# A new order of work in a fused attention and expert kernel: the next rows' transposes in two visits around the last up block, and the sixth expert product behind the query product

## The chip, the cores and the metric

The kernel runs on one core of a Trainium2 chip. The metric is the device time of one execution in microseconds (us). Runs of the kernel before gave 1293.66, 1293.72 and 1294.25 us, median 1293.72 us. Engine names are those of the profile: PE (matmul), PEld (its weight load), DVE (vector), ACT (scalar), POOL (GpSimd), SP (queues of the DMAs).

## The reference

For each of 32 batch rows ("turns" below) of 256 tokens by 256 features and 77 context tokens:

```
latents = layernorm(x); ctx = masked context
q = LN(latents) @ W_q;  k, v = [LN(ctx), LN(latents)] @ W_kv      # 333 keys, 4 heads of 64
x1 = x + softmax(rms(q) rms(k)^T / 8) v @ W_out + b_out
h  = layernorm(x1)
cw = router(h)                        # sigmoid, best of 2 groups, 2 of 8 experts
out = x1 + shared(h) + sum_e cw[e] * relu(h @ up[e])^2 @ down[e]  # all 8 experts are computed
```

All of it is in float32. The kernel splits each operand of a large product into a high and a low part (`_hi`, `_lo`) and adds three products: hi*hi, hi*lo, lo*hi.

## The kernel before

Five engines each run a program of their own, written out by hand, and meet only in semaphores. A turn `step(b, ...)` holds the attention of row b, the router and experts of row b-1 (`ffn(...)`, `high`, `add`, `routing`, `low`) and the layer norm and projections of row b+1 (the lines under `if following`). No scheduler moves anything: an engine does what its `step` lists, in that order, and stops at a `wait_ge` until it is met. 31 turns have experts, 30 of those also prepare a next row. After the last turn a drain computes the experts of the last row alone.

What the names stand for on PE: `transpose_k`, `sum_q_squares` open the turn; `up(p)` (p = 0 to 5) computes two hidden blocks into bank p % 2 of `up_ps`; `shared` and `down(e)` are the products back to 256 features in `down_ps`; `score_pair`, `transpose_probs(u)`, `probs_times_v` are the attention; `transpose_ln(b + 1)` turns the normalized next rows `x_hat`, `c_hat` into `up_ps` (feature half ft = 0 in bank 0, ft = 1 in bank 1); `spread_inverse` transposes the softmax's inverse sums; `project_kv`, `project_out`, `project_q` are the projections and `transpose_x2` opens the second layer norm's output to the experts.

The chain of an `up` block runs over four engines: ACT reads the bank (`relu_sb`, line 657) and squares it (`relu2`, 662), DVE rounds it to `hid_hi` (981, `high(p)`), POOL subtracts (`hid_lo`, 1176, `low(p)`), then PE may use it in `down`. `down(e)` for e = 2, 3 needs `high(3)` and `low(3)`. Its result is added up by DVE (`add(e)`, 996), and `down(e)` waits until `add(e - 2)` has freed the bank.

The chain of the next rows: DVE takes the statistics (`layer_norm1`, 740 to 758), POOL the inverse root (`rstd_first`, 1133, which stands behind `low(3)` on POOL), DVE writes `x_hat`, `c_hat` (`normalize1`, 765, 767), PE transposes them (275, 276), ACT applies gain and bias (`ln_full`, 576), DVE and POOL split (775, 1144), and `project_kv` starts.

At the turn's end DVE computes `x1` from the output projection (872), its statistics, the key norms (795, 800), `x2_hat` (891), the normalized keys `k_rms` (810), which `transpose_k` of the next turn waits for, and `x2_lo` (898), which `up(0)` waits for.

## Time and profile before

| | before |
|---|---|
| median of three runs | 1293.72 us |
| the profiled execution's own time | 1296.0 us |
| its span, first to last instruction | 1294.1 us |
| PE busy | 1218.2 us (94% of the span) |
| DVE busy | 1048.6 us (81%) |
| ACT busy | 752.5 us (58%) |
| POOL busy | 539.6 us (42%) |
| mean granted clock of PE | 0.989 |
| one turn in the middle (start of `transpose_k` to the next) | 38.96 us |

The span is what the sums of this document are made against; the profiled execution took 1.9 us more than its span. Busy time of PE is modelled from pipelined matmuls, so a PE that shows 94% is not idle for the other 6% alone. The granted clock of PE was nine tenths or more in every slice of the page but the second (7) and the last (8), so it tells no stretch of the middle apart. The turns repeat each other to a few hundredths of a microsecond. One turn, 645.34 to 684.30 us, stands for all in what follows.

### The profile page before, as it was taken

The numbers are of one execution on the slowest core, as the hardware profiler recorded it, in microseconds if no ns is written. First come the engines' busy times: TensorE is split into PE (matmuls) and PEld (weight loads), VectorE is DVE, ScalarE is ACT, GpSimd is POOL, SyncE is SP. The second block draws the span as 40 slices with busy tenths as digits, with TensorE's granted clock in tenths as the row PEclk, the third lists the DMA queues.
The fourth block names the chain that finished last, engine by engine and source line by source line (L and its number), as shares of the span: only waits on it lengthen the run. The fifth ranks groups of instructions, "written<-read, shape, count | busy, mean of one in ns | idle before, by whom it ended". The sixth has DMA issues, their size and how long they took to land.

```text
span 1294.1 us, 29594 instructions
## 1 busy us (share of the span) xinstructions
PE 1218.2 (94%) x10176; PEld 1105.8 (85%) x10176; DVE 1048.6 (81%) x3561; ACT 752.5 (58%) x1733; POOL 539.6 (42%) x477
## 2 busy tenths in 40 slices
PE   3799999999999999999999999999999999999987
PEld 2589888889888888888888888888888888988876
DVE  3778888888888888888888888888888888888875
ACT  3566556666555666556656556656556566555652
POOL 3244454344344344444344444344444344344332
PEclk9799999999999999999999999999999999999998
DMA  4000000000000000000000000000000000000000
GB/s 145 12 12 21 20 20 10 12 21 20 21 20 16 5 21 20 20 20 20 2 21 20 20 20 20 2 21 20 20 20 20 2 21 21 20 20 20 2 9 17
DMA packets 28227, 25.84 MB, mean 20 GB/s; under 512 B 6640, under 2 KB 27536, under 8 KB 28080
## 3 DMA queue, kind: packets, MB, share of 16 engines
q1 hardware_dynamic: 27744, 23.83, 5.8%
q8 instruction: 82, 1.34, 0.4%
q0 software_dynamic: 336, 0.14, 0.2%
q14 instruction: 65, 0.53, 0.1%
HBM read 15.57 MB, written 8.39 MB: 19 GB/s over the span
## 4 chain that ended last, share of the span: by engine, by line
PE 60%; DVE 18%; issue 14%; ACT 7%; POOL 1%; DMA 1%; DVEq 0%; POOLq 0%; ACTq 0%
PE up_ps L261 8%; PE up_ps L263 7%; PE attn_ps L370 7%; PE up_ps L262 7%; PE attn_ps L356 4%; PE attn_ps L261 4%; PE down_ps L261 4%; DVE masked L830 4%; PE attn_ps L262 3%; PE attn_ps L263 3%; ACT relu L662 3%; PE down_ps L262 3%; PE down_ps L263 3%; ACT relu_sb L657 3%; DVE acc L996 2%
## 5 line engine op out<-in xcount | busy, mean ns | idle before, releaser
L1176 POOL TENSOR_TENSOR hid_lo<-relu,hid_hi 128x512 fp32r<-128x512 f32 x192 | 247.3, 1288 | 417.1 <-DVE hid_hi L981 417.1
L261 PE MATMUL down_ps<-down_hi,hid_hi 128*128 128x256 f32 x768 | 236.1, 307 | 5.1 <-issue 3.0
L996 DVE SCALAR_TENSOR_TENSOR acc<-down_ps,route_w,acc 128x256 f32<-128x256 f32 x512 | 221.6, 475 | 13.9 <-PE down_ps L263 13.5
L261 PE MATMUL up_ps<-x_hi,up_hi 128*128 128x256 f32 x768 | 227.7, 296 | 3.4 <-issue 0.4
L262 PE MATMUL down_ps<-down_lo,hid_hi 128*128 128x256 f32 x768 | 216.3, 282 | 0.0
L263 PE MATMUL down_ps<-down_hi,hid_lo 128*128 128x256 f32 x768 | 216.1, 281 | 0.0
L262 PE MATMUL up_ps<-x_lo,up_hi 128*128 128x256 f32 x768 | 216.1, 281 | 0.0
L263 PE MATMUL up_ps<-x_hi,up_lo 128*128 128x256 f32 x768 | 215.7, 281 | 0.0
L617 ACT ACTIVATE probs<-masked,neg_max,q_scale 128x333 f32<-128x333 f32 x256 | 168.3, 658 | 73.7 <-DVE neg_max L837 73.7
L657 ACT ACTIVATE relu_sb<-up_ps 128x512 f32<-128x512 f32 x192 | 114.6, 597 | 105.8 <-PE up_ps L263 99.2
L981 DVE CAST hid_hi<-relu 128x512 fp32r<-128x512 f32 x192 | 124.6, 649 | 56.6 <-ACT relu L662 56.4
L261 PEld LDWEIGHTS down_ps<-down_hi,hid_hi 128*128 128x128 f32 x768 | 145.7, 190 | 19.5 <-issue 17.6
L261 PEld LDWEIGHTS up_ps<-x_hi,up_hi 128*128 128x128 f32 x768 | 146.4, 191 | 18.1 <-issue 13.2
L262 PEld LDWEIGHTS down_ps<-down_lo,hid_hi 128*128 128x128 f32 x768 | 145.9, 190 | 1.2
L262 PEld LDWEIGHTS up_ps<-x_lo,up_hi 128*128 128x128 f32 x768 | 146.0, 190 | 0.0
L263 PEld LDWEIGHTS up_ps<-x_hi,up_lo 128*128 128x128 f32 x768 | 145.8, 190 | 0.0
L263 PEld LDWEIGHTS down_ps<-down_hi,hid_lo 128*128 128x128 f32 x768 | 145.4, 189 | 0.0
L624 ACT ACTIVATE up_stage<-attn_ps 111x384 f32<-111x384 f32 x256 | 117.8, 490 | 43.6 <-PE attn_ps L356 43.5
L1133 POOL TENSOR_TENSOR rstd<-var,minus_half 128x2 f32<-128x2 f32 (+1 forms) x64 | 51.4, 803 | 204.2 <-DVE var L884 191.7
L662 ACT ACTIVATE relu<-relu_sb 128x512 f32<-128x512 f32 x192 | 121.3, 632 | 6.1
L356 PE MATMUL attn_ps<-ident,probs 128*111 128x128 f32 x768 | 117.1, 283 | 7.9 <-DVE row_max L830 7.9
L830 DVE CUSTOM_DVE_ANT_0 masked<-attn_ps,mask_row 128x333 f32<-128x333 f32 x256 | 118.1, 498 | 0.3 <-issue 0.3
(147 smaller groups left out, 2821.5 us busy)
## 6 DMA issues: line engine op xcount, KB each, us to landing
x_in<-in_x SPq DMA_DIRECT2D x32, 256.0 KB, 2.8
out<-acc SPq DMA_DIRECT2D x32, 256.0 KB, 2.1
c_in<-in_ctx SPq DMA_DIRECT2D x32, 77.0 KB
up_stage<-in_up_t SPq DMA_DIRECT2D x1, 1536.0 KB, 12.9
down_stage<-in_down_t SPq DMA_DIRECT2D x1, 1536.0 KB, 15.3
mask_in<-in_mask SPq DMA_DIRECT2D x32, 9.6 KB, 2.6
w_stage<-in_w_kv SPq DMA_DIRECT2D x1, 512.0 KB, 5.8
w_stage<-in_w_q SPq DMA_DIRECT2D x1, 256.0 KB, 5.0
```

The lines of the kernel that those rows point to most:

```text
L261: nc.tensor.matmul(out_ap, s_hi, m_hi, start=first, stop=False)
L262: nc.tensor.matmul(out_ap, s_hi, m_lo, start=False, stop=False)
L263: return nc.tensor.matmul(out_ap, s_lo, m_hi, start=False, stop=last)
L356: last = nc.tensor.transpose(attn_ps[0:KC, u % PT_RING, c * P:(c + 1) * P], probs[:, u, c * KC:(c + 1) * KC], ident[:])
L617: nc.scalar.activation(probs[:, u, :], masked[:, u, :], ACT.Exp, bias=neg_max[:, u:u + 1], scale=q_scale[:, u:u + 1], accum_out=row_sum[:, ...
L624: nc.scalar.activation(probs_t[:, u % PT_SB, :], attn_ps[0:KC, u % PT_RING, 0:CH * P], ACT.Copy).then_inc(pt_done, 1)
L657: nc.scalar.activation(relu_sb[:, p % 2, :], up_ps[:, p % 2, :], ACT.Relu).then_inc(relu_done, 1)
L662: nc.scalar.activation(relu2[:, p % 2, :], relu_sb[:, p % 2, :], ACT.Square).then_inc(relu2_done, 1)
L830: nc.vector.tensor_tensor_reduce(masked[:, u, :], attn_ps[:, u % SCORE_RING, 0:KEYS], mask_row[:], 1.0, -MASKED, ALU.add, ALU.max, row_max ...
L981: nc.vector.tensor_copy(hid_hi[:, p % HID_RING, :], relu2[:, p % 2, :]).then_inc(hid_hi_done, 1)
L996: nc.vector.scalar_tensor_tensor(acc[:, t, :], down_ps[:, (e + 1) % 2, t * D:(t + 1) * D], route_w[:, t, e:e + 1], acc[:, t, :], ALU.mult, ...
L1176: nc.gpsimd.tensor_tensor(hid_lo[:, p % HID_RING, :], relu2[:, p % 2, :], hid_hi[:, p % HID_RING, :], ALU.subtract).then_inc(hid_lo_done, 1)
```

## The change

Nothing is computed differently but two things are cut finer: the output projection of token half t now goes to bank t of `up_ps`, signals each half, and DVE adds the residual in two halves (`residual_half`); and `transpose_ln` and `ln_full` take one feature half at a visit. Everything else is order. On PE: the router ahead of `up(1)`; score pairs 0 and 1 together and 2 and 3 together; `up(2)`, `up(3)` adjacent; probability transposes 0, 1, 2 together, 4, 5, 6 together; `down(1)` ahead of `probs_times_v`; the next rows' first half transposed ahead of `up(5)`, the second half behind `down(3)`; two of three `project_kv` ahead of `project_out`; `down(5)` behind `project_q`, which now waits for the first residual half. ACT, DVE and POOL follow with orders of their own.

```diff
-            def transpose_ln(b, experts):
+            def transpose_ln(b, ft, experts):
+                if ft == 0:
+                    pe.wait_ge(x_hat_done, b + 1)
...
             def project_q(b):
-
+                if not (isinstance(b, int) and b == 0):
+                    pe.wait_ge(x1_done, (b - 1) * T + 1)
...
-                    last = split_product(up_ps[:, 1, t * D:(t + 1) * D], (at_hi[:, k, cols], at_lo[:, k, cols]),
+                    last = split_product(up_ps[:, t, 0:D], (at_hi[:, k, cols], at_lo[:, k, cols]),
...
-                if t == T - 1:
-                    last.then_inc(out_ps, 1)
+                last.then_inc(out_ps, 1)
...
                 ffn("up", 0)
-                ffn("up", 1)
                 if experts:
                     router(f)
+                ffn("up", 1)
                 score_pair(b, 0, experts)
+                score_pair(b, 1, experts)
                 ffn("up", 2)
-                score_pair(b, 1, experts)
                 ffn("up", 3)
                 score_pair(b, 2, experts)
+                score_pair(b, 3, experts)
                 ffn("shared", 0)
                 ffn("shared", 1)
-                score_pair(b, 3, experts)
                 transpose_probs(b, 0)
                 transpose_probs(b, 1)
+                transpose_probs(b, 2)
                 ffn("down", 0)
-                transpose_probs(b, 2)
                 transpose_probs(b, 3)
                 ffn("up", 4)
+                ffn("down", 1)
                 probs_times_v(b, 0)
                 probs_times_v(b, 1)
-                ffn("down", 1)
                 transpose_probs(b, 4)
                 transpose_probs(b, 5)
+                transpose_probs(b, 6)
                 ffn("down", 2)
+                if following:
+                    transpose_ln(b + 1, 0, experts)
                 ffn("up", 5)
-                transpose_probs(b, 6)
                 ffn("down", 3)
                 if following:
-                    transpose_ln(b + 1, experts)
+                    transpose_ln(b + 1, 1, experts)
...
                 if following:
                     project_kv(b + 1, 1)
-                ffn("down", 5)
+                    project_kv(b + 1, 2)
                 project_out(b, 0, following)
                 project_out(b, 1, following)
                 if following:
-                    project_kv(b + 1, 2)
                     project_kv(b + 1, 0)
                     project_q(b + 1)
+                ffn("down", 5)
                 ffn("down", 6)
...
+            def residual_half(b, t):
+                if t == 0:
+                    dve.wait_ge(x_res_done, b + 1)
+                dve.wait_ge(out_ps, b * T + t + 1)
+                nc.vector.tensor_tensor(x1[:, t, :], up_ps[:, t, 0:D], x_res[:, t, :], ALU.add).then_inc(x1_done, 1)
+                dve.wait_ge(x1_done, b * T + t + 1)
+                nc.vector.bn_stats(stats2[:, t, :], x1[:, t, :]).then_inc(ln2_step, 1)
...
                 high(0)
-                high(1)
                 routing(0)
...
                 mask_scores(b, 0, first)
                 mask_scores(b, 1, first)
-                routing(1, 2, 3, 4, 5, 6)
                 mask_scores(b, 2, first)
                 mask_scores(b, 3, first)
-                routing(7)
                 negate_max(b, 0)
-                routing(8)
-                high(2)
-                routing(9, 10)
+                high(1)
+                routing(1, 2, 3, 4, 5, 6, 7, 8)
                 mask_scores(b, 4, first)
                 mask_scores(b, 5, first)
-                routing(11, 12)
+                high(2)
+                mask_scores(b, 6, first)
+                mask_scores(b, 7, first)
+                negate_max(b, 1)
+                routing(9, 10, 11, 12)
...
                 widen_inverse(b, 0, first)
+                high(4)
                 if following:
                     normalize1(b + 1, False)
                 add(1)
-                high(4)
-                add(2)
-                high(5)
-                add(3)
                 invert_sums(b, 1)
                 widen_inverse(b, 1, first)
+                add(2)
+                add(3)
                 if following:
                     ln_high(b + 1, False)
+                high(5)
                 add(4)
                 attn_out(b, first)
                 attn_low(b, 0)
                 attn_low(b, 1)
+                if following:
+                    k_norms(b + 1, 0, False)
+                residual_half(b, 0)
+                residual_half(b, 1)
+                layer_norm2(b, first)
+                if following:
+                    k_norms(b + 1, 1, False)
+                normalize2(b, first)
                 add(5)
...
                 low(4)
+                if following:
+                    ln_low(b + 1)
                 low(5)
                 if following:
-                    ln_low(b + 1)
+                    k_scales(b + 1, 0, False)
                 rstd_second(b, first)
```

How the rows move is shown at three places. The first is DVE behind the fourth masked score tile, before the change: `neg_max` frees ACT for the softmax, CAST is `high(2)`, `in_group` to `tied` are router levels.

```order
L939 TENSOR_TENSOR group_sum<-top1,top2 128x4
L837 SCALAR_TENSOR_TENSOR neg_max<-row_max,q_scale 128x4
L942 TENSOR_TENSOR group_sel<-group_sum 128x2
L944 TENSOR_TENSOR group_sel<-group_sum 128x2
L981 CAST hid_hi<-relu2 128x512
L947 TENSOR_TENSOR in_group<-biased,group_sel 128x16
L952 TENSOR_TENSOR above<-in_group 128x128
L953 TENSOR_TENSOR tied<-in_group 128x128
```

The same place with the change (its lines are numbered a few higher); CAST is now `high(1)`:

```order
L842 SCALAR_TENSOR_TENSOR neg_max<-row_max,q_scale 128x4
L987 CAST hid_hi<-relu2 128x512
L929 TENSOR_SCALAR sig_den<-exp_neg 128x16
L931 RECIPROCAL score<-sig_den 128x16
L933 TENSOR_TENSOR biased<-score,gbias 128x16
L936 TENSOR_TENSOR pair_hi<-biased 128x8
```

`high(1)` has moved from ahead of the masked scores to behind `neg_max`, and router levels 1 to 8 now run in one piece directly behind it; `high(2)` and levels 9 to 12 come later still.

The second place is PE around the last `up` block. Before, from the last matmul of `down(3)`'s first half on; L356 is `transpose_probs(7)`:

```order
L263 MATMUL down_ps<-down_hi,hid_lo 128x256
L261 MATMUL down_ps<-down_hi,hid_hi 128x256
L262 MATMUL down_ps<-down_lo,hid_hi 128x256
L263 MATMUL down_ps<-down_hi,hid_lo 128x256
L275 MATMUL up_ps<-ident,x_hat 128x128 x2
L276 MATMUL up_ps<-ident,c_hat 128x77
L275 MATMUL up_ps<-ident,x_hat 128x128 x2
L276 MATMUL up_ps<-ident,c_hat 128x77
L356 MATMUL attn_ps<-ident,probs 111x128 x3
```

With the change, the first visit stands between `down(2)` and `up(5)`, which follows in twelve matmuls (three are shown):

```order
L263 MATMUL down_ps<-down_hi,hid_lo 128x256
L273 MATMUL up_ps<-ident,x_hat 128x128 x2
L274 MATMUL up_ps<-ident,c_hat 128x77
L261 MATMUL up_ps<-x2_hi,up_hi 128x256
L262 MATMUL up_ps<-x2_lo,up_hi 128x256
L263 MATMUL up_ps<-x2_hi,up_lo 128x256
```

and the second behind `down(3)`:

```order
L262 MATMUL down_ps<-down_lo,hid_hi 128x256
L263 MATMUL down_ps<-down_hi,hid_lo 128x256
L273 MATMUL up_ps<-ident,x_hat 128x128 x2
L274 MATMUL up_ps<-ident,c_hat 128x77
L355 MATMUL attn_ps<-ident,probs 111x128 x3
```

So the wait for `x_hat` and `c_hat` has moved ahead of `up(5)` (12 matmuls) and `down(3)` (6 matmuls), and `transpose_probs(6)`, which stood between those two, is gone from there.

The third place is DVE around `normalize1`. Before:

```order
L996 SCALAR_TENSOR_TENSOR acc<-down_ps,route_w,acc 128x256 x2
L850 COPY inv_wide<-row_inv 128x256
L765 TENSOR_SCALAR x_hat<-x_in,mv1,rstd1 128x256 x2
L767 TENSOR_SCALAR c_hat<-c_in,mv1,rstd1 77x256
L996 SCALAR_TENSOR_TENSOR acc<-down_ps,route_w,acc 128x256 x2
L981 CAST hid_hi<-relu2 128x512
```

With the change:

```order
L1002 SCALAR_TENSOR_TENSOR acc<-down_ps,route_w,acc 128x256 x2
L855 COPY inv_wide<-row_inv 128x256
L987 CAST hid_hi<-relu2 128x512
L770 TENSOR_SCALAR x_hat<-x_in,mv1,rstd1 128x256 x2
L772 TENSOR_SCALAR c_hat<-c_in,mv1,rstd1 77x256
L1002 SCALAR_TENSOR_TENSOR acc<-down_ps,route_w,acc 128x256 x2
```

`high(4)` has moved ahead of `x_hat`; POOL's `low(4)` waits for it and stands behind `rstd_first`.

## Rows read from the trace of the kernel before

**Rows 1.** Page, part 4: the chain that ended last, by engine.
```profile
PE 60%; DVE 18%; issue 14%; ACT 7%; POOL 1%; DMA 1%; DVEq 0%; POOLq 0%; ACTq 0%
```

**Rows 2.** The waits of 100 to 1200 us, longest first.
```profile
PE up_ps L386 <- DVE inv_wide L850: 17.8, 28, 0.7
...
PE attn_ps L356 <- DVE row_max L830: 7.4, 28, 0.5
```

**Rows 3.** Timeline of PE in one row's turn: start, length (us), operation.
```profile
645.34 0.76 PE L321 MATMUL attn_ps<-ident,k_rms 111*128 111x111 f32 x6
...
650.68 0.42 PE L342 MATMUL attn_ps<-k_hi,q_hi 64*128 64x334 f32 x2
...
651.09 0.32 PE L346 MATMUL attn_ps<-k_hi,q_lo 64*128 64x334 f32 x2
651.33 0.39 PE L261 MATMUL up_ps<-x_hi,up_hi 128*128 128x256 f32 x1
...
652.94 0.42 PE L342 MATMUL attn_ps<-k_hi,q_hi 64*128 64x334 f32 x2
...
661.73 0.88 PE L356 MATMUL attn_ps<-ident,probs 128*111 128x128 f32 x6 [0.50 <-DVE row_max L830]
...
667.55 0.29 PE L261 MATMUL up_ps<-x_hi,up_hi 128*128 128x256 f32 x1
...
672.48 0.66 PE L386 MATMUL up_ps<-ident,inv_wide 128*128 128x128 f32 x4 [0.64 <-DVE inv_wide L850]
673.06 1.53 PE L370 MATMUL attn_ps<-up_stage,v_sb 111*64 111x128 f32 x24
...
683.51 0.37 PE L261 MATMUL down_ps<-down_hi,hid_hi 128*128 128x256 f32 x1
684.18 0.28 PE L263 MATMUL down_ps<-down_hi,hid_lo 128*128 128x256 f32 x1
684.30 0.73 PE L321 MATMUL attn_ps<-ident,k_rms 111*128 111x111 f32 x6
```

**Rows 4.** Timeline of DVE, the same turn.
```profile
651.29 1.35 DVE L981 CAST hid_hi<-relu 128x512 fp32r<-128x512 f32 x1 [0.31 <-ACT relu L662]
...
653.52 0.52 DVE L923 TENSOR_SCALAR sig_den<-exp_neg 128x16 f32<-128x16 f32 x1
...
656.82 0.43 DVE L981 CAST hid_hi<-relu 128x512 fp32r<-128x512 f32 x1 [0.20 <-issue]
...
657.37 1.40 DVE L952 TENSOR_TENSOR above<-in_group 128x128 f32<-128x128 f32 x1
```

**Rows 5.** Timeline of POOL, the same turn.
```profile
651.06 1.29 POOL L1176 TENSOR_TENSOR hid_lo<-relu,hid_hi 128x512 fp32r<-128x512 f32 x1 [0.36 <-DVE hid_hi L981]
...
657.33 1.29 POOL L1176 TENSOR_TENSOR hid_lo<-relu,hid_hi 128x512 fp32r<-128x512 f32 x1 [3.33 <-DVE hid_hi L981]
```

**Rows 6.** Timeline of DVE, statistics and rows of the next turn.
```profile
662.42 0.74 DVE L740 BATCH_NORM_STATS2 stats<-x_in 128x6 f32<-128x256 f32 x2
...
666.95 0.74 DVE L765 TENSOR_SCALAR x_hat<-x_in,mv,rstd 128x256 f32<-128x256 f32 x2 [0.75 <-POOL rstd L1133]
667.60 0.40 DVE L767 TENSOR_SCALAR c_hat<-c_in,mv,rstd 77x256 f32<-77x256 f32 x1
```

**Rows 7.** Timeline of POOL, the next rows' inverse root.
```profile
666.00 0.92 POOL L1133 TENSOR_TENSOR rstd<-var,minus_half 128x3 f32<-128x3 f32 x1
```

**Rows 8.** One line's instructions (L765): duration ns min/median/max.
```profile
L765 DVE TENSOR_SCALAR x_hat<-x_in,mv,rstd x64: 403/410/417, 14.8 to 1208.7; 128x256 f32<-128x256 f32 x64
```

**Rows 9.** Timeline of ACT, two releases.
```profile
669.18 0.60 ACT L657 ACTIVATE relu_sb<-up_ps 128x512 f32<-128x512 f32 x1 [0.95 <-PE up_ps L263]
...
679.79 0.60 ACT L594 ACTIVATE k_sq<-attn_ps 111x512 f32<-111x512 f32 x1 [3.64 <-PE attn_ps L263]
```

**Rows 10.** Timeline of DVE, the residual sum.
```profile
678.40 0.69 DVE L872 TENSOR_TENSOR x<-up_ps,x_res 128x512 f32<-128x512 f32 x1 [0.54 <-PE up_ps L263]
```

**Rows 11.** Timeline of POOL, the second inverse root.
```profile
680.44 0.69 POOL L1133 TENSOR_TENSOR rstd<-var,minus_half 128x2 f32<-128x2 f32 x1 [5.93 <-DVE var L884]
```

More of the change, by code:

```diff
@@ L263, in split_product @@
                 return nc.tensor.matmul(out_ap, s_lo, m_hi, start=False, stop=last)
-            def transpose_ln(b, experts):
-                pe.wait_ge(x_hat_done, b + 1)
-                if not (isinstance(b, int) and b == 0) and not experts:
-                    pe.wait_ge(q_lo_done, b)
-                for ft in range(FT):
-                    if experts:
-                        pe.wait_ge(relu_done, (b - 2) * PAIRS + PAIRS - 1 + ft)
-                    for t in range(T):
-                        nc.tensor.transpose(up_ps[:, ft, t * P:(t + 1) * P], x_hat[:, t, ft * P:(ft + 1) * P], ident[:])
-                    nc.tensor.transpose(up_ps[:, ft, S:KEYS], c_hat[:, ft * P:(ft + 1) * P],
-                                        ident[0:C, 0:C]).then_inc(lnt_ps, 1)
+            def transpose_ln(b, ft, experts):
+                if ft == 0:
+                    pe.wait_ge(x_hat_done, b + 1)
+                    if not (isinstance(b, int) and b == 0) and not experts:
+                        pe.wait_ge(q_lo_done, b)
+                if experts:
+                    pe.wait_ge(relu_done, (b - 2) * PAIRS + PAIRS - 1 + ft)
+                for t in range(T):
+                    nc.tensor.transpose(up_ps[:, ft, t * P:(t + 1) * P], x_hat[:, t, ft * P:(ft + 1) * P], ident[:])
+                nc.tensor.transpose(up_ps[:, ft, S:KEYS], c_hat[:, ft * P:(ft + 1) * P],
+                                    ident[0:C, 0:C]).then_inc(lnt_ps, 1)
             def project_q(b):
+                if not (isinstance(b, int) and b == 0):
+                    pe.wait_ge(x1_done, (b - 1) * T + 1)
                 for ft in range(FT):
@@ L566, in split_hi, with ln_full @@
                 nc.scalar.activation(dst, src, ACT.Copy).then_inc(w_hi_done, 1)
-            def ln_full(b, first):
+            def ln_full(b, fts, first):
                 if not first:
@@ L572, in ln_full @@
                     act.wait_ge(ln_lo_done, b * FT)
-                for ft in range(FT):
+                for ft in fts:
                     act.wait_ge(lnt_ps, b * FT + ft + 1)
@@ L676, in step @@
                     split_hi(2, down_hi[:], down_stage[:])
[L677 removed]
                 if experts:
                     router_exp(f, f_first)
+                ffn(1)
+                softmax(b, 0, first)
+                softmax(b, 1, first)
                 ffn(2)
[L681 to L682 removed]
+                softmax(b, 2, first)
+                softmax(b, 3, first)
+                ffn(3)
+                softmax(b, 4, first)
                 pt_out(b, 0, first)
[L684 removed]
                 pt_out(b, 1, first)
                 pt_out(b, 2, first)
[L687 removed]
+                softmax(b, 5, first)
                 pt_out(b, 3, first)
[L689 removed]
+                softmax(b, 6, first)
                 ffn(4)
[L691 removed]
+                softmax(b, 7, first)
                 pt_out(b, 4, first)
[L693 removed]
                 pt_out(b, 5, first)
+                pt_out(b, 6, first)
+                if following:
+                    ln_full(b + 1, (0,), False)
                 ffn(5)
                 if following:
[L697 to L698 removed]
+                    ln_full(b + 1, (1,), False)
                 pt_out(b, 7, first)
@@ L713, in _ @@
             act.wait_ge(vectors_in, 10 * DMA)
-            ln_full(0, True)
+            ln_full(0, range(FT), True)
             for part in range(2):
@@ L865, in attn_low @@
                                         ALU.subtract).then_inc(at_lo_done, 1)
+            def residual_half(b, t):
[5 more added lines that the diff above has]
+                nc.vector.bn_stats(stats2[:, t, :], x1[:, t, :]).then_inc(ln2_step, 1)
             def layer_norm2(b, first):
                 k = b * LN2_STEPS
-                dve.wait_ge(out_ps, b + 1)
-                dve.wait_ge(x_res_done, b + 1)
-                nc.vector.tensor_tensor(x1[:], up_ps[:, 1, :].rearrange("p (t d) -> p t d", d=D), x_res[:],
-                                        ALU.add).then_inc(x1_done, 1)
-                dve.wait_ge(x1_done, b + 1)
-                for t in range(T):
-                    nc.vector.bn_stats(stats2[:, t, :], x1[:, t, :]).then_inc(ln2_step, 1)
                 dve.wait_ge(ln2_step, k + T)
```

31 lines of the change are left out of this document (7 added, 24 removed).

## The prediction

> **What bounds the kernel now.** I read the page's chain first: PE holds 60% of what ended last and DVE 18% [rows 1], and PE is busy 94% of the span. So the time is PE's program plus the places where PE stops. The waits say where it stops in the middle of the run: for `inv_wide` ahead of `spread_inverse` and for the masked scores ahead of `transpose_probs(2)`, once a turn each [rows 2]. Then the timeline of one turn: it takes 684.30 - 645.34 = 38.96 us [rows 3]. I write K for its start at 645.34 and V for 673.06, where `probs_times_v(2)` begins. The printed waits are 0.50 and 0.64 us, counted from the modelled end of the last matmul, 0.28 after its start; where nothing waits, the next block starts 0.12 after it (684.18, 684.30). So the two stops cost about 0.65 and 0.79, together 1.44 us a turn. That is the most the change can win by removing waits: 30 x 1.44 = 43 us.
>
> **The change on PE, by durations.** Every matmul is still issued. A score pair with an up block behind it takes 0.65 (650.68 to 651.33) and an up block between two pairs 1.61; the first matmul after a switch is 0.39 long, not 0.28 [rows 3]. Two pairs side by side and two up blocks side by side save three such switches, each some 0.1 to 0.2: I take 0.5 in all (range 0.2 to 0.6). The router between two up blocks gives 0.1 of it back, the grouped transposes win 0.1. PE's own work shrinks from 38.96 - 1.44 = 37.5 to 37.0 us a turn.
>
> **The two old stops.** `transpose_probs(2)` now starts about K+14.3 and needs the seventh masked tile, which I place at K+13 (below): gone. `inv_wide` is now made ahead of `add(2)`, `add(3)` and the last rounding, about 2 us before PE asks: gone.
>
> **What is late next: `x_hat`.** The first transposes of the next rows now stand ahead of `up(5)`. PE would be there at K+21.2: before, `up(5)` began at 667.55 = K+22.21 [rows 3], less 0.65 (stop), less 0.6 (switches), plus 0.25 for `transpose_probs(6)`, moved ahead of it. Before, the same transposes came 2.5 us after that point. When is `c_hat`, which signals both, ready?
>
> DVE rows first [rows 4]. Before, from the start of `high(1)` at 651.29 (K+5.95) to the statistics at 662.42 (K+17.08) [rows 6] there are 11.13 us. 0.20 of it is idle. The rest holds blocked time: `high(1)` took 1.35, `above` 1.40, `sig_den` 0.52, where the same cast took 0.43 at 656.82 and tiny operations 0.17. `hid_lo` on POOL began at 651.06 and 657.33 and took 1.29 [rows 5]; `high(1)`, issued in the middle of it, ended 0.29 behind it, and `above` 0.15 behind it. I read that a DVE operation that reads two tiles of SBUF, or the cast, stands still while `hid_lo` runs. Excess: 0.92 + 0.35 + 1.1 (`above` undisturbed taken as 0.3). Work is 11.13 - 0.20 - 2.37 = 8.55.
>
> With the change, the same work less the logits' 0.1 starts at the first masked tile. Score pair 0 starts at K+5.34 before (650.68) and K+5.5 now, its last matmul ends 0.73 later (651.09 + 0.32) [rows 3]: mask at K+6.25. 6.25 + 8.45 = 14.7. Router levels that used to be laced with masked tiles now follow one another, each waiting for the last one's end (`in_group` to `above`: some 0.04 to 0.1 exposed): about ten places, 0.4. Two blocks on POOL remain: `high(1)` is issued at K+8.16 (four tiles, then `neg_max`), so `low(1)` runs K+8.7 to 9.95 and catches `biased`, wanted at 9.0: 0.95. `high(2)` ends at K+12.5, `low(2)` runs to 13.9 and catches `in_group`, wanted at 13.5: 0.4. Sum 14.7 + 0.4 + 0.95 + 0.4 = K+16.45 for the statistics, 0.6 earlier than before. From their start (662.42) to the end of `c_hat` (667.60 + 0.40) were 5.58 [rows 6], through `high(3)`, `low(3)` and the inverse root of 0.92 on POOL [rows 7]; nothing in that stretch is shortened. Ready at K+22.05, PE goes at K+22.1. **New stop: 0.9 us.** Bounds: 0 if neither small operation is blocked (1.35 earlier), 1.3 if the gaps are double.
>
> **From there to the next turn.** Before, `up(5)` to the next K took 684.30 - 667.55 = 16.75. Less 0.79 (stop) and 0.25 (`transpose_probs(6)`) leaves 15.7. Added are three small waits. (a) The second visit needs ACT to have read `up(5)`'s bank: that read started 0.20 after the block's end (669.18) [rows 9] and takes 0.60, and only `down(3)`, 0.7, lies between now: 0.13 (range 0 to 0.3). (b) `high(5)` now stands between the second `ln_hi` and POOL's second `ln_lo`, which the first `project_kv` needs: 0 to 0.2, I take 0.1. (c) `down(7)` needs `add(5)`, which stood early and now stands behind `x2_hat`. The second `project_kv` starts 2.1 earlier, so its squares (679.79 [rows 9]) come at V+4.6, `k_sum` and `k_norm` end for DVE at V+6.05. The residual halves follow. Before, `x1` to POOL's root took 680.44 - 678.40 = 2.04 [rows 10, 11]; in halves I add 0.15: V+8.25. Root 0.69, `x2_hat` from V+9.0, `add(5)` V+9.65 to 10.5. PE wants `down(7)` at V+10.45 (683.51) [rows 3]: 0.13 (range 0 to 0.4). `k_rms` follows at V+11.1, `transpose_k` is wanted at V+11.4: just covered, and with 0.3 less on either side it would be the next stop. `down(5)` itself moves at no cost: it waits for nothing late, and the residual's first half (V+6.5) is ready before `project_q` wants its bank (V+7.25). DMAs keep their places; the next rows' load is released by `x_res`, which ends about K+5.2, 11 us ahead of the statistics.
>
> **Sum.** 22.1 + 15.7 + 0.13 + 0.1 + 0.13 = 38.15 us a turn, against 38.96: 0.8 less. 30 turns: 24 us. The last turn with experts has no next rows; it loses the stop at `transpose_probs(2)` and some switches: 1 us. The first turn and the drain stay. 1294.1 - 25 = 1269 us of span; the runs' median, 1293.72, lies 0.4 below the span, so 1268.5 us.
>
> **A rule weighed.** `high(4)` now ends just ahead of `x_hat`, so POOL starts `low(4)` as soon as its root is out, at the moment in which DVE starts `x_hat`. `x_hat`'s 64 instructions took 403 to 417 ns for 256 elements, never more [rows 8], while the cast moves 512 elements in 0.43 and was held up by `hid_lo` [rows 4, 5]. `x_hat` never ran beside `hid_lo` before, so no row shows whether it would be held. I take it as free. The Trainium skill, SBUF — State Buffer, section Who interferes with whom, says that a DVE instruction holds the port pair that it shares with GpSimd if it has two SBUF inputs or runs in a 2-port mode, that `tensor_scalar` can enter such a mode, and that whoever starts first holds the pair to its end. By VectorE: DVE Perf Modes, section What auto-detection actually checks, a single source and destination in SBUF suffice, and `x_hat` is of that form. By the first rule the blocked rows here are explained; by both, `x_hat` would be blocked as well, which is the rival (3) below; its 403 ns at half the cast's elements speak against that.
>
> **Rivals.**
> (1) `x_hat` is in time, because `biased` and `in_group` are not blocked or DVE has more slack than I see. For it: no such small two-input row stood beside `hid_lo` in the turn that I read except those two that did wait. Then the stop of 0.9 goes: 37.25 a turn, 1.7 less, 51 + 1 = 52 us: 1241 us.
> (2) The tail turns late: `add(5)`, `k_rms` and the second `ln_lo` each 0.15 to 0.3 later than I place them, 0.4 to 0.6 more a turn: 38.65, 10 us won: 1283 us. They all sit within 0.3 us of PE's demand.
> (3) `x_hat` is held by `low(4)`. POOL's 1.29 comes ahead of it, so the first transposes start at K+23.4. 39.45 a turn, 0.5 more than before: 15 - 1 = 14 us: 1307 us, slower. It decides from 0.8 us of holding on.
> (4) Nothing measurable: the new stops together cost what the old ones did, 0.8 us above my sum.
>
> **How the numbers follow.** My forecast 0.55 (its own range 1256 to 1280), (1) 0.14, (2) 0.15, (3) 0.11, (4) 0.05. A measurement of this kernel tells 0.2% (2.6 us) from no change. Faster: 0.55 + 0.14 + 0.15 less a little of (2) that reaches too far = 0.82; same 0.05; slower 0.13. The range leaves out half of (1), and (3): 1242 to 1291.
>
> **What would show it.** In the profile after: no wait at `transpose_probs(2)` and at `spread_inverse`; a wait of PE for `c_hat` ahead of the first transposes in 30 turns, 0.6 to 1.2 us each (0: rival 1; 2: rival 3, with `x_hat` over 1 us); `biased` about 1.1 us long; small waits for `relu_sb` and for `acc` ahead of `down(7)`. If the turn shortens by under 0.5 us although `c_hat` waits 0.9, the tail is what I mis-sized.

## The result, and the profile after

The change made the kernel slower: 1323.03 us (median of four runs, 1318.26 to 1325.54) against 1293.99 us for the kernel before on the same chip (four runs, 1293.66 to 1295.81). The ratio is 1.0217, 95% interval 1.0187 to 1.0247. Forecast were 1268.5 us, range 1242 to 1291. The span of the profiled execution is 1323.7 us.

Page of the changed kernel, parts 1 and 4 and the clock line of part 2, in tenths of full speed:

```profile
PE 1222.1 (92%) x10176; PEld 1127.2 (85%) x10176; DVE 1056.4 (80%) x3593; ACT 751.4 (57%) x1733; POOL 539.1 (41%) x477
...
PEclk9799999999999999999999999999999999999998
...
PE 48%; issue 24%; POOL 9%; DVE 9%; ACT 8%; DMA 1%; ACTq 0%; POOLq 0%; DVEq 0%
POOL hid_lo L1180 6%; PE up_ps L261 5%; PE up_ps L263 5%; PE up_ps L262 5%; PE down_ps L261 4%; PE attn_ps L261 4%; PE attn_ps L369 4%; PE attn_ps L262 3%; ACT probs L618 3%; PE attn_ps L263 3%; PE down_ps L262 3%; PE down_ps L263 3%; ACT relu_sb L658 2%; POOL rstd L1137 2%; PE up_ps L273 2%
```

POOL held 1% of the chain before [rows 1], now 9%, 6% of it in `hid_lo`. That share is not the cause itself. In the turn shown below the chain holds the `hid_lo` of 431.71 and that of 437.96, which stand ahead of the next rows' inverse root, and the time in which `x_hat` is held by the next `hid_lo` goes by the name of `issue`:

```profile
437.96 1.28 POOL hid_lo L1180
439.24 0.88 POOL rstd L1137
440.34 1.07 issue
```

The waits of PE from 100 to 1200 us say where the two old ones [rows 2] went (total us, times, longest):

```profile
PE up_ps L273 <- DVE c_hat L772: 48.6, 27, 1.9
PE attn_ps L261 <- issue: 1.5, 7, 0.3
```

The old stops are gone, as forecast, and one new stop is there, where it was forecast, but of 1.8 us and not 0.9. The same place on three engines, in the turn that starts at K = 419.36 (start, length, operation; in brackets the idle time before it and what ended it). DVE:

```profile
428.16 1.00 DVE L933 TENSOR_TENSOR biased<-score,gbias 128x16 f32<-128x16 f32 x1
...
435.61 0.75 DVE L745 BATCH_NORM_STATS2 stats<-x_in 128x6 f32<-128x256 f32 x2
...
440.14 1.68 DVE L770 TENSOR_SCALAR x_hat<-x_in,mv,rstd 128x256 f32<-128x256 f32 x2 [0.42 <-POOL rstd L1137]
441.74 0.40 DVE L772 TENSOR_SCALAR c_hat<-c_in,mv,rstd 77x256 f32<-77x256 f32 x1
```

POOL:

```profile
439.19 0.91 POOL L1137 TENSOR_TENSOR rstd<-var,minus_half 128x3 f32<-128x3 f32 x1
440.08 1.26 POOL L1180 TENSOR_TENSOR hid_lo<-relu,hid_hi 128x512 fp32r<-128x512 f32 x1
```

PE:

```profile
440.12 0.28 PE L263 MATMUL down_ps<-down_hi,hid_lo 128*128 128x256 f32 x1
442.19 0.44 PE L273 MATMUL up_ps<-ident,x_hat 128*128 128x128 f32 x2 [1.79 <-DVE c_hat L772]
...
442.94 0.31 PE L261 MATMUL up_ps<-x_hi,up_hi 128*128 128x256 f32 x1
443.06 0.41 PE L262 MATMUL up_ps<-x_lo,up_hi 128*128 128x256 f32 x1
443.26 0.41 PE L263 MATMUL up_ps<-x_hi,up_lo 128*128 128x256 f32 x1
```

`hid_lo` starts 0.06 ahead of `x_hat`, and the two `x_hat` take 1.68 together, where they took 0.74 [rows 6]: rival (3), with 0.94 of holding. The inverse root, also a `tensor_tensor` on POOL (128x3, 0.91 us), held nobody: the cast at 439.31, which ran beside it, took 0.42, as alone. Over the whole program the line that answers to [rows 8] reads:

```profile
L770 DVE TENSOR_SCALAR x_hat<-x_in,mv,rstd x64: 399/408/1355, 14.5 to 1240.3; 128x256 f32<-128x256 f32 x64
```

The median hides it, since only the first of each pair is held; the longest, 1355 ns, shows it.

The second thing was not forecast at all. From 443.06 on matmuls of one shape start 0.21 apart and no longer 0.12 (rows above). The table by stretches of 2 us (length, then busy us and instructions of PE, PEld, DVE, ACT, POOL, then the granted clock of PE as a share of 2.4 GHz, then the DMAs):

```profile
440.00:442.00 2.00, 0.40 (x4) 0.20 (x2) 1.86 (x3) 0.33 (x1) 1.34 (x2) 1.00 0.00 0
442.00:444.00 2.00, 1.80 (x12) 1.81 (x13) 1.97 (x7) 0.87 (x2) 0.00 (x0) 0.76 0.03 8
444.00:446.00 2.00, 2.00 (x11) 2.00 (x11) 0.12 (x1) 0.97 (x2) 0.00 (x0) 0.50 0.00 0
446.00:448.00 2.00, 2.00 (x18) 1.96 (x16) 1.39 (x4) 1.43 (x4) 0.53 (x1) 0.88 0.00 0
```

Behind the stop PE runs at the lower of its two levels, 1.2 GHz, for some 3 us. That happens in 18 of the 30 turns: those take 40.38 us on average, the other 12 take 38.93 in the median. How often it happens differs from one execution to the next: the four executions of this kernel had a mean clock of 0.968, 0.969, 0.968 and 0.975 and took 1325.54, 1322.99, 1323.06 and 1318.26 us. The page's clock line cannot show it: a slice there is 33 us, from whose mean 3 us at half speed take 0.05, and a 9 stands for nine tenths or more.

The turns of before, measured between starts of `transpose_k` over the whole trace, have a median of 38.67 us; the one that the prediction was worked out on, 38.96, is the second longest. That turns repeat each other to a few hundredths, as said ahead of the prediction, holds for most and not for all. The mean over the 30 turns after the first is 38.74 before and 39.81 with the change: 1.07 x 30 = 32 us more; the first turn is 1.4 longer and the rest 4 shorter, which makes the 29.6 us between the spans. The 1.4 is no price of the change: the two kernels with filler matmuls below differ in nothing that the first turn runs, and it took 34.01 us in one and 35.71 in the other.

The longest turn of before, its second, shows the lower clock as well. PE paused for 0.86 us ahead of it and for 0.31 us 2 us later, the granted clock fell at about the time of the second pause, and the turn took 40.15, 1.48 over the median, in part from longer waits:

```profile
63.63 1.12 PE L321 MATMUL attn_ps<-ident,k_rms 111*128 111x111 f32 x6 [0.86 <-DVE k_rms L810]
...
65.86 0.55 PE L261 MATMUL up_ps<-x_hi,up_hi 128*128 128x256 f32 x1 [0.31 <-DVE x_lo L898]
...
64.00:66.00 2.00, 1.59 (x14) 1.32 (x13) 1.95 (x6) 0.98 (x3) 0.17 (x1) 0.88 0.03 8
66.00:68.00 2.00, 2.00 (x10) 2.00 (x11) 0.70 (x2) 0.00 (x0) 2.00 (x2) 0.50 0.00 0
```

### The profile page after: what moved, and what is told of

Its sections match the earlier page's. It is cut to its first block, busy times and chain, and to the rows that moved or that the text cites. A ratio compares the mean times of both kernels' runs of the same rounds, so it can differ in the third digit from the quotient of the medians.

```text
span 1323.7 us, 29657 instructions
## 1 busy us (share of the span) xinstructions
PE 1222.1 (92%) x10176; PEld 1127.2 (85%) x10176; DVE 1056.4 (80%) x3593; ACT 751.4 (57%) x1733; POOL 539.1 (41%) x477
## 3 DMA queue, kind: packets, MB, share of 16 engines
q8 instruction: 83, 1.36, 0.4%
## 4 chain that ended last, share of the span: by engine, by line
PE 48%; issue 24%; POOL 9%; DVE 9%; ACT 8%; DMA 1%; ACTq 0%; POOLq 0%; DVEq 0%
POOL hid_lo L1180 6%; PE up_ps L261 5%; PE up_ps L263 5%; PE up_ps L262 5%; PE down_ps L261 4%; PE attn_ps L261 4%; PE attn_ps L369 4%; PE attn_ps L262 3%; ACT probs L618 3%; PE attn_ps L263 3%; PE down_ps L262 3%; PE down_ps L263 3%; ACT relu_sb L658 2%; POOL rstd L1137 2%; PE up_ps L273 2%
## 5 line engine op out<-in xcount | busy, mean ns | idle before, releaser
L261 PE MATMUL up_ps<-x_hi,up_hi 128*128 128x256 f32 x768 | 233.7, 304 | 0.2 <-DVE x_lo L904 0.2
L263 PE MATMUL down_ps<-down_hi,hid_lo 128*128 128x256 f32 x768 | 221.3, 288 | 0.0
L263 PE MATMUL up_ps<-x_hi,up_lo 128*128 128x256 f32 x768 | 221.2, 288 | 0.0
L261 PEld LDWEIGHTS down_ps<-down_hi,hid_hi 128*128 128x128 f32 x768 | 151.3, 197 | 19.2 <-issue 19.2
L262 PEld LDWEIGHTS up_ps<-x_lo,up_hi 128*128 128x128 f32 x768 | 151.4, 197 | 0.0
L262 PEld LDWEIGHTS down_ps<-down_lo,hid_hi 128*128 128x128 f32 x768 | 151.2, 197 | 0.0
L1148 POOL TENSOR_TENSOR ln_lo<-ln_t,ln_hi 128x333 fp32r<-128x333 f32 x64 | 60.9, 952 | 188.9 <-DVE ln_hi L780 188.9
L1137 POOL TENSOR_TENSOR k_scale<-k_norm,minus_half 111x8 f32<-111x8 f32 x64 | 84.7, 1324 | 118.4 <-DVE k_norm L805 118.4
L625 ACT ACTIVATE up_stage<-attn_ps 111x384 f32<-111x384 f32 x256 | 110.9, 487 | 21.8 <-PE attn_ps L355 21.8
L987 DVE CAST hid_hi<-relu 128x512 fp32r<-128x512 f32 x192 | 97.2, 506 | 25.6 <-ACT relu L663 25.3
```

Source lines behind the costliest of these rows:

```text
L261: nc.tensor.matmul(out_ap, s_hi, m_hi, start=first, stop=False)
L262: nc.tensor.matmul(out_ap, s_hi, m_lo, start=False, stop=False)
L263: return nc.tensor.matmul(out_ap, s_lo, m_hi, start=False, stop=last)
L625: nc.scalar.activation(probs_t[:, u % PT_SB, :], attn_ps[0:KC, u % PT_RING, 0:CH * P], ACT.Copy).then_inc(pt_done, 1)
L987: nc.vector.tensor_copy(hid_hi[:, p % HID_RING, :], relu2[:, p % 2, :]).then_inc(hid_hi_done, 1)
L1137: nc.gpsimd.tensor_tensor(dst, src, minus_half[0:src.shape[0], 0:src.shape[1]], ALU.pow).then_inc(done, 1)
```

## The experiments

Theory A: `x_hat` is held by `hid_lo` of `low(4)`, which lengthens the stop to 1.8 us, and the long stop costs clock as well. Rivals: the lower clock has a cause of its own and would stay (B), or the new order loses elsewhere, in the tail of the turn with the moved `down(5)` (C). Later there are a rival D, whatever is removed, the next late thing takes its place, and a rival E, something else in the new order makes `x_hat` slow. Edits are to the changed kernel unless said otherwise. Turn lengths are medians between starts of `transpose_k`, as above. Ratios are to the kernel before on the same chip, where its median was between 1294.02 and 1296.21 us.

### x_hat ahead of the rounding

```diff
-                high(4)
                 if following:
                     normalize1(b + 1, False)
+                high(4)
                 add(1)
```

> The changed kernel with one line moved back: the fifth rounding (high(4)) stands behind x_hat and c_hat again, so POOL's low(4) cannot run beside x_hat. Theory (A): half of PE's stop before the first transposes is x_hat held by low(4) (two x_hat 1.68 us against 0.74), the other half is the longer chain, and a stop of nearly 2 us brings PE's granted clock down behind it. Then x_hat takes 0.74 for two, the stop shrinks from 1.8 to about 0.9 us, and the undisturbed turn from 38.93 to 38.0 us. If a stop of 0.9 us leaves the clock alone: all windows 1.00, 1272 to 1278 us. If it does not: 1300 to 1312 us. Rival (B), the low clock has a cause of its own: about 28 us less than the change, no more (1295 us), with the clock as low as before. Rival (C), the loss is in the turn's tail (sixth product, halves of the residual): no change, 1318 us or more.

Measured: 1271.38 us (1270.13 to 1272.78), ratio 0.9818 (0.9802 to 0.9834); the turn is 37.97 us, and none has a lower clock. Waits and `x_hat` (from 100 to 1200 us; busy us, mean ns):

```profile
PE up_ps L273 <- DVE c_hat L772: 24.6, 29, 1.0
...
L770 DVE TENSOR_SCALAR x_hat<-x_in,mv,rstd 128x256 f32<-128x256 f32 x58 | 21.3, 410 | 21.8 <-POOL rstd L1137 21.8
```

One line moved by two places is worth 51.7 us: 3.9% of the kernel. The stop is 0.85, the forecast's 0.9, and `x_hat` starts where it did (20.75 us into the turn, 20.78 in the change), so the difference is the hold alone. A holds and B falls. The 51.7 us are about 29 of hold (30 turns of 38.93 against 37.97) and 22 of clock.

### The clock by itself

Filler matmuls of 256 columns, whose result nobody reads, keep PE at work in the stop; `x_hat` stays held.

```diff
             def transpose_ln(b, ft, experts):
+                if ft == 0 and experts:
+                    pe.wait_ge(relu_done, (b - 2) * PAIRS + PAIRS - 1)
+                    for _ in range(12):
+                        nc.tensor.matmul(up_ps[:, 0, 0:S], up_hi[:, 0, 0:P], x2_hi[:, 0, :], start=True, stop=True)
```

> The changed kernel, and ahead of the wait for x_hat PE computes 12 matmuls of 256 columns into the bank that the transposes overwrite; their result is used by nothing. x_hat stays held by low(4), so the transposes start no earlier. Theory (A), the stop brings the clock down: PE is busy for about 1.4 of the 1.8 us, the granted clock is 1.00 in all windows of the middle, and every turn takes the 38.9 us that the turns with full clock take now: 1302 us (1298 to 1306). Rival (B), the clock falls for another reason: it still falls in two turns of three, 1320 us or more. This prices the clock apart from the wait.

Measured: 1301.13 us (1300.82 to 1302.31), ratio 1.0053 (1.0038 to 1.0068). The stop's end does not move and no turn of the 30 has a lower clock; their median is 38.95 (the longest 39.32), the length of the 12 undisturbed ones of the change:

```profile
397.55 1.58 PE L269 MATMUL up_ps<-x_hi,up_hi 128*128 128x256 f32 x12
399.56 0.44 PE L277 MATMUL up_ps<-ident,x_hat 128*128 128x128 f32 x2 [0.43 <-DVE c_hat L776]
```

Useless work makes the kernel 22 us faster: that is the price of the clock. With `range(4)`:

> As the kernel with 12 filling matmuls, with 4: PE is busy for 0.5 us of the stop and waits about 1.3. If the low clock follows a long enough stop (theory A), it comes less often than the 18 turns of 30 in the change and more often than in none: 1301 to 1315 us. If 4 fillers leave as many low turns as none (1318 us or more), the length of the stop is not what decides.

Measured: 1301.36 us (1300.92 to 1302.29), ratio 1.0045 (1.003 to 1.006), median turn 38.95. Four fillers shorten the pause to some 1.35 and are enough; some low turns were expected, none came:

```profile
399.98 0.44 PE L277 MATMUL up_ps<-ident,x_hat 128*128 128x128 f32 x2 [1.36 <-DVE c_hat L776]
```

### The hold alone, in the kernel before

```diff
                 widen_inverse(b, 0, first)
+                high(4)
                 if following:
                     normalize1(b + 1, False)
                 add(1)
-                high(4)
```

> The kernel before with one line moved: high(4) ahead of x_hat and c_hat, as in the change. DVE was idle 0.75 us there, so the rounding itself fits in. If a rounding on POOL running beside x_hat holds it (theory A), the two x_hat take 1.6 to 1.7 us instead of 0.74 here too, add(1) behind them comes 0.9 later and down(3) waits for its bank: 0.4 to 0.8 us a turn, 1306 to 1318 us. Rival (E), x_hat's 1.68 us in the changed kernel come from something else in the new order (the store or load of rows, ACT): x_hat stays 0.74 and the time stays at 1292 to 1296 us, or gains.

Measured: 1304.06 us (1302.61 to 1305.44), ratio 1.0064 (1.0049 to 1.0079), turn 38.96 against 38.67:

```profile
L765 DVE TENSOR_SCALAR x_hat<-x_in,mv,rstd 128x256 f32<-128x256 f32 x56 | 47.8, 893 | 11.7 <-POOL rstd L1133 11.7
...
PE down_ps L261 <- DVE acc L996: 12.1, 28, 0.7
```

The same hold (893 ns on average) comes with no other part of the change, and slows that kernel too. That leaves no room for E. It costs 0.3 a turn, less than the low end expected. PE asks for `x_hat` 2.5 us later there, and what is late is `add(1)`, queued behind `x_hat`. The 0.3 is a difference: the edit also put the rounding into a stretch in which DVE was idle, and the old stop for `inv_wide` (17.8 us in all, [rows 2]) is no longer among the waits.

### down(5) back

```diff
+                ffn("down", 5)
                 project_out(b, 0, following)
...
                     project_q(b + 1)
-                ffn("down", 5)
                 ffn("down", 6)
```

with `add(5)` back ahead of `k_norms` on DVE.

> The changed kernel with the sixth expert product back ahead of the output projections and its add(5) back ahead of the key norms; all else as changed. Theory (A): this part of the change neither wins nor loses more than 0.2 us a turn; the stop before the first transposes and the low clock stay: 1315 to 1326 us. Rival (C), the sixth product behind the query product loses: 10 us or more faster than the change.

Measured: 1320.14 us (1318.23 to 1324.76), ratio 1.0203 (1.018 to 1.0226). The undisturbed turn is 39.32 against 38.93, so the move of `down(5)` gains 0.4 a turn, more than the 0.2 expected, and C falls. The gain has a row: with `down(5)` early, PE reaches `transpose_x2` too soon.

```profile
PE up_ps L273 <- DVE c_hat L772: 50.4, 28, 1.9
PE attn_ps L408 <- DVE x_hat L897: 11.9, 28, 0.4
```

That the total hardly moved has another cause: the stop for `c_hat` is as long as in the change, but only 7 turns of 30 have the lower clock behind it, not 18.

### The transposes at their old place

Both visits behind `down(3)` on PE and both `ln_full` behind `ffn(5)` on ACT; `x_hat` stays held.

```diff
                 ffn("down", 2)
-                if following:
-                    transpose_ln(b + 1, 0, experts)
                 ffn("up", 5)
                 ffn("down", 3)
                 if following:
+                    transpose_ln(b + 1, 0, experts)
                     transpose_ln(b + 1, 1, experts)
```

> The changed kernel with both halves of the next rows' transposes behind down(3) again, in one visit, on PE and ACT; all else as changed. Theory (A): x_hat is still held by low(4) and c_hat is ready at K+22.8, but PE asks at K+23.4, so the stop is gone, the clock stays at 1.00, and what the rest of the new order wins shows: a turn of 37.2 to 37.8 us (the second ln_lo may now be late for the projections), 1255 to 1270 us. Rival (C), the tail or another part of the new order loses time too: above 1280 us.

Measured: 1292.49 us (1290.34 to 1293.69), ratio 0.9982 (0.9972 to 0.9991), turn 38.67. The loss against the kernel before is gone, but hardly anything is won, and the time lies in the range of rival C. What took the place of the stop is in the rows:

```profile
PE down_ps L261 <- DVE acc L999: 35.8, 28, 1.4
PE attn_ps L261 <- issue: 14.8, 28, 0.7
```

The stop at `x_hat` is gone, and `down(3)`, which now comes before it, waits 1.26 for `add(1)`, which stands behind the held `x_hat` on DVE. So one edit more, on top of this one:

```diff
                 high(4)
+                add(1)
                 if following:
                     normalize1(b + 1, False)
-                add(1)
```

> The kernel with both visits at their old place, and add(1) ahead of x_hat and c_hat on DVE. There down(3) waited 1.3 us for add(1), behind the held x_hat. Theory (A'): the held x_hat was the cause of that wait as well; with add(1) ahead the wait is gone, c_hat comes at about K+23.0 and is wanted at K+23.4: a turn of 37.3 to 37.9 instead of 38.66, 1252 to 1272 us. Rival (D), the new order carries another second of waiting that moves along whatever is done: 1285 us or more.

Measured: 1251.38 us (1250.04 to 1252.31), ratio 0.966 (0.9644 to 0.9676), turn 37.31. So it was no other part of the new order that lost. `x_hat` is still held in all 30 turns, and nobody waits for it. The hold is shorter: `x_hat` starts 0.35 us behind `hid_lo` there and takes 1.09, in the change 0.06 behind and 1.36, and both times it ends 0.15 behind `hid_lo`. Over the middle of the run (busy us, mean ns), and the longest wait of PE:

```profile
L767 DVE TENSOR_SCALAR x_hat<-x_in,mv,rstd 128x256 f32<-128x256 f32 x58 | 41.1, 749 | 0.0
...
PE attn_ps L261 <- issue: 11.2, 29, 0.6
```

### The first visit one block later

`x_hat` free as in the first experiment, and the first visit between `up(5)` and `down(3)`.

> The changed kernel with high(4) behind x_hat again and the first visit of the transposes between up(5) and down(3) instead of ahead of up(5) (ACT reads both halves behind its sixth hidden block). Theory (A), all that is lost is the wait for c_hat and what follows from it: c_hat is ready at about K+21.9 and PE asks at K+22.3, so the stop of 0.84 is gone, the clock stays up, a wait of up to 0.3 us of down(3) for add(1) or of the projections for ln_lo may appear: a turn of 37.1 to 37.4 us, 1243 to 1254 us. Rival (D), the time only moves to the next stop, as when both visits stood at their old place: 1265 us or more.

Measured: 1259.62 us (1258.25 to 1259.88), ratio 0.9719 (0.9705 to 0.9734), turn 37.54. Again `down(3)` waits for `add(1)`, 0.35 a turn, and the gain over the first experiment is 12 us, where 17 at least were expected. Hence the last group.

### Three moves together, and who is held

The first visit between `up(5)` and `down(3)`, and on DVE `add(1)`, then `x_hat`, then `high(4)`:

> The change with three moves together: add(1) ahead of x_hat on DVE, high(4) behind x_hat and c_hat, and the first visit of the transposes between up(5) and down(3) on PE. Theory (x_hat free again, first visit asked for 1.6 us later, down(3)'s bank freed ahead of x_hat): no stop of PE is left there, the turn is about 37.1 us against 37.54 with the last two moves alone, which had a stop of 0.35 to 0.5 for add(1): 1243 to 1252 us, clock 1.00 in every turn. Rival (PE has reached the next latest thing, as in three runs so far): c_hat, now 0.7 us later behind add(1), or ln_lo ahead of project_kv takes the stop over and the turn stays at 37.4 to 37.6: 1254 to 1260 us.

Measured: 1264.33 us (1262.66 to 1264.69), ratio 0.9755 (0.9742 to 0.9768), turn 37.71: slower than the last two kernels (1251.38, 1259.62), and beyond both ranges. With the same order on DVE and both visits at the old place:

> The change with the DVE order add(1), x_hat and c_hat, high(4) and both visits behind down(3) on PE. With x_hat held (add(1), high(4), x_hat) the same PE order gave 37.30 us a turn and 1251.4 us, with one stop of 0.4 to 0.6 left at project_kv for ln_lo. Theory: x_hat was not what bound that kernel, but x_hat free by 0.9 us brings the next rows' products forward only if their chain (transposes, ln_full, split) is what project_kv waits for: since the transposes stand where PE reaches them and not where x_hat is ready, no change: 1249 to 1254 us. Rival: the chain of ln_lo does start from x_hat: 0.3 to 0.5 us a turn less, 1236 to 1243 us.

Measured: 1263.7 us (1263.1 to 1265.99), ratio 0.9756 (0.9742 to 0.9769), turn 37.73. It differs from the 1251.4 us kernel only in that `high(4)` stands behind `x_hat`, which frees `x_hat`, and it is 12 us slower. Its rows:

```profile
L852 DVE COPY inv_wide<-row_inv 128x256 f32<-128x256 f32 x58 | 55.9, 964 | 1.0
L767 DVE TENSOR_SCALAR x_hat<-x_in,mv,rstd 128x256 f32<-128x256 f32 x58 | 21.4, 411 | 0.0
...
427.39 1.40 DVE L852 COPY inv_wide<-row_inv 128x256 f32<-128x256 f32 x1
428.71 1.65 DVE L999 SCALAR_TENSOR_TENSOR acc<-down_ps,route_w,acc 128x256 f32<-128x256 f32 x4
...
427.36 1.29 POOL L1177 TENSOR_TENSOR hid_lo<-relu,hid_hi 128x512 fp32r<-128x512 f32 x1 [1.51 <-DVE hid_hi L984]
...
429.73 0.35 PE L261 MATMUL down_ps<-down_hi,hid_hi 128*128 128x256 f32 x1 [0.52 <-DVE acc L999]
```

The hold was not removed but handed on: `hid_lo` starts at 427.36 and holds the copy to `inv_wide` at 427.39 (1.40, else 0.29), behind it `add(2)` is late, and `down(4)` waits for that. With `high(5)` behind `add(4)` on top of the three moves:

> The kernel with the three moves, and high(5) behind add(4) on DVE, so that POOL's ln_lo no longer waits for or is stretched by it. If ln_lo ahead of project_kv is the stop that is left: 0.2 to 0.4 us a turn less than with the three moves alone, 1236 to 1248 us. If down(5) or down(6) then waits for hid_lo of the last block, or nothing waited for ln_lo: the same within 3 us, or slower.

Measured: 1261.77 us (1260.96 to 1262.44), ratio 0.9738 (0.9725 to 0.9751), turn 37.64: 2.6 us less, within the 3 of the second case. The waits of PE for an addition stayed (13.9 us before, 14.0 with it), and `inv_wide`'s second copy takes up to 1.40 us in both kernels, as in the one above; that hold was not touched. The last kernel takes the one with both visits at the old place and a free `x_hat`, and puts nothing behind `high(4)` that can be held:

```diff
-                high(4)
                 invert_sums(b, 1)
                 widen_inverse(b, 1, first)
+                high(4)
                 add(2)
```

> The kernel with both visits behind down(3) and x_hat free, with the second inverse sums and inv_wide moved ahead of high(4) on DVE, so that nothing that reads SBUF alone stands between high(4) and add(2), add(3), and hid_lo of block 4 on POOL finds no one to hold. Theory (one hold of about 1.1 us goes to whichever SBUF-only DVE operation stands behind high(4): x_hat, inv_wide; the additions, which read PSUM, are not held): inv_wide's second copy takes 0.29 again instead of 1.40, add(2) is done 0.9 us earlier, down(4)'s stop of 0.52 goes: 37.1 to 37.25 us a turn against 37.73, 1243 to 1249 us; if the next rows' ln_hi, ln_lo come earlier too and the 0.32 at project_kv goes with it, 36.85, 1236 to 1243. Rival: hid_lo of block 4 starts 0.4 later and down(4) waits for it in place of add(2), or the hold falls on another operation that PE waits for: 37.5 to 37.8, 1255 to 1265 us.

Measured: 1250.83 us (1249.6 to 1251.42), ratio 0.9663 (0.9649 to 0.9676), turn 37.26. The four additions behind `high(4)` run beside `hid_lo` at their usual pace, and the copy is short:

```profile
424.35 1.29 POOL L1177 TENSOR_TENSOR hid_lo<-relu,hid_hi 128x512 fp32r<-128x512 f32 x1 [1.92 <-DVE hid_hi L984]
...
424.19 1.66 DVE L999 SCALAR_TENSOR_TENSOR acc<-down_ps,route_w,acc 128x256 f32<-128x256 f32 x4
...
L852 DVE COPY inv_wide<-row_inv 128x256 f32<-128x256 f32 x58 | 23.7, 409 | 1.0
...
PE attn_ps L261 <- issue: 11.7, 29, 0.6
```

The stop of 0.52 is gone, and 0.40 ahead of `project_kv` is left. The time is 2 us above the first of the two ranges expected. One more hold stands in the chain ahead of it, which no run took away: the second `ln_hi` runs beside the first `ln_lo` and takes 0.81 instead of 0.34.

```profile
426.73 0.90 POOL L1145 TENSOR_TENSOR ln_lo<-ln_t,ln_hi 128x333 fp32r<-128x333 f32 x1 [1.08 <-DVE ln_hi L777]
...
427.00 0.81 DVE L777 CAST ln_hi<-ln_t 128x333 fp32r<-128x333 f32 x1 [0.35 <-ACT ln_t L576]
```

This kernel and the one with `add(1)` ahead of a held `x_hat` (1251.38) cannot be told apart; both beat the change by some 72 us and the kernel before by 3.4%.

## Why the prediction was wrong

- **The failed step** is "I take it as free", under A rule weighed. It rested on two readings of `x_hat`'s rows: that it was never longer than 417 ns, which said nothing, since `hid_lo` never ran beside it, and that 403 ns at half the cast's elements looked like an operation in no fast mode, hence one that holds no port. The second was an inference from speed to port, and it is false: `x_hat` takes 410 ns when free and 1355 when `hid_lo` is ahead of it. By the Trainium skill, SBUF — State Buffer, section Who interferes with whom, with VectorE: DVE Perf Modes, section What auto-detection actually checks, an operation of `x_hat`'s form is held by a GpSimd operation that started first; the changed kernel's trace agrees, with 0.94 us a turn. The experiment that moves `high(4)` alone gives back 51.7 us, and lands at 1271.4, 2.9 from the forecast; how much of that nearness is luck is said under the base. The trace of before had the answer for another operation of the same kind. `sig_den` is a `tensor_scalar` too, from one SBUF tile to another; in [rows 4] it takes 0.52 instead of 0.17, and the prediction counted the 0.35 as blocked time, though its own reading (two tiles of SBUF, or the cast) doesn't cover it. It ended 0.03 behind this `hid_lo`:

```profile
652.72 1.29 POOL L1176 TENSOR_TENSOR hid_lo<-relu,hid_hi 128x512 fp32r<-128x512 f32 x1 [0.36 <-DVE hid_hi L981]
```

- **The rival that came true** was priced too low: 39.45 a turn, 1307 us. As a turn it was too high (38.93 at full clock). What it lacked is the lower clock behind a pause of 1.8 us: 18 turns x 1.44 = 26 us by turn lengths, 22 by the fillers. No row of before had a pause of PE over 0.7 us in the middle turns [rows 2], but the trace of before had the lower clock at its second turn, around two pauses of 0.86 and 0.31 us, with the matmuls there 0.21 apart. What could not be read was how often a pause of 1.8 is followed by it. The clock should have stood as an unknown of that rival, in the range's upper end.
- **Right:** both old stops went. `biased` was held (1.00; forecast "about 1.1"), and the statistics came at K+16.25 (forecast 16.45), though by another way: `in_group` was not held, `neg_max` ahead of it took 0.50. The stop for `c_hat` without the hold is 0.85 (0.9). From the first transposes to the next turn 403.25 to 419.36 = 16.11 us passed in an undisturbed turn (forecast 15.7 and 0.36 of small waits). Of these no wait for `relu_sb` or for `add(5)` shows, only 1.5 us in all at `project_kv`. `down(5)` "at no cost" was too cautious; its old place costs 0.4 a turn.
- **The base:** 38.15 forecast against 37.97 measured without the hold is good, but it was set against a turn of 38.96 where the median is 38.67. The turn that was read had the longest stop for the masked scores, 0.50; the mean is 0.26 (7.4 us in 28, [rows 2]). So the gain from the old stops was overstated by some 0.25 a turn. The small waits, 0.36, were overstated too: without the hold only 0.06 shows. These two errors go opposite ways, so that 0.8 a turn was forecast and 0.7 measured; that part of the nearness is luck. PE's own work shrank as forecast: without its stops, each counted 0.15 longer as in the prediction, the median turn is 38.67 - 0.26 - 0.64 - 0.30 = 37.5 before and 37.97 - 0.85 - 0.15 = 37.0 after.
- **In the experiments** the expectation failed in one way three times (transposes at the old place, one block later, three moves together): a stop was removed and the whole of it booked as gain, though the next late operation in the same queue (`add(1)` behind `x_hat`, `add(2)` behind `inv_wide`) stood less than the gain behind. The fourth of these misses, at 1263.7, took the hold for gone when it was only handed on.

What stays open: why 18 turns with a pause of 1.8 us are followed by the lower clock and 12 are not, and why with `down(5)` at its old place it is 7 and 23. Among these the length of the pause does not decide it, since pauses of 1.74 to 1.84 stand ahead of the undisturbed turns and of 1.78 to 1.90 ahead of the others, and both kernels are known by one profiled execution each, while the mean clock differs between executions of one kernel. Whether the last hold, that of `ln_hi`, costs anything was not tested.

## What to carry to other kernels

Before a rounding is moved on DVE, look at what its follower on POOL will run beside: a large POOL `tensor_tensor` over SBUF (`hid_lo`, 1.29 us) held whichever stood next of `x_hat`, `inv_wide`, `biased`, `neg_max`, `sig_den` and the casts, and did nothing to additions that read PSUM, nor to the reciprocals; so put the PSUM readers behind the release, and expect a hold that is moved to fall on the next in the queue. That an operation was never slow where nothing ran beside it is no evidence that it can't be held: give such a step an even chance, and the larger price. A stop of PE of 1.8 us was followed, in 18 of 30 turns of one kernel and 7 of 30 of another, by a lower clock that cost another 1.3 to 1.4 us, which only stretches of a few microseconds show.

## What the runs showed of the hardware

- A `tensor_scalar` of 128x256 in float32, 410 ns alone, and a copy of that size, 290 ns alone, are held by a `tensor_tensor` of 128x512 on POOL that starts a few hundredths earlier, up to 1355 ns and 1400 ns, and end 0.15 us behind it. A reciprocal of 128x16 from SBUF to SBUF that started 0.04 behind the same operation (427.88, in the changed kernel) took 0.25, as alone. The small `tensor_tensor` of the inverse root on POOL (128x3, 0.91 us) did not hold a cast of 128x512 beside it (0.42). Four additions with one operand in PSUM took 1.66 us beside the 128x512 `tensor_tensor`, and 1.65 where it had ended before them.
- With one pause of PE of about 0.4, 0.85 or 1.35 us a turn none of 30 turns had a lower clock. The second turn of before had, with pauses of 0.86 and 0.31 us about it. With 1.8 us 18 of 30 had in one kernel and 7 of 30 in another, for some 3 us each, at 0.41 instead of 0.28 us per matmul as the profile models its length, 0.21 instead of 0.12 from start to start.
- A few matmuls without a reader in a pause of PE (four, which shortened it from 1.8 to 1.35 us) were enough to keep the clock: 22 us of 1323 won by added work.
